# Top-two routing: one-hots laid out with the token tiles innermost, 16-bit operands, number tables repeated by GpSimd

## The chip, the cores and the metric

One core of one Trainium2 chip runs the whole program in one launch. The metric is the device time of one execution in microseconds, the median over the runs.

## The reference

The model is a chain of four gated attention layers, each followed by a gated feed-forward layer, over x of shape 2 x 1024 x 256. The change touches the last feed-forward layer, a mixture of 8 experts of which every token uses its best two:

```python
router_logits = x @ wg.T                       # 2048 tokens, 8 experts
probs = softmax(router_logits)
topk_w, topk_idx = top_k(probs, 2)
topk_w = topk_w / sum(topk_w)
expert_w = sum(one_hot(topk_idx, 8) * topk_w[..., None], axis=1)
h1 = einsum('th,eih->tei', x, w1)
h3 = einsum('th,eih->tei', x, w3)
y = einsum('tei,ehi->teh', silu(h1) * h3, w2)
out = einsum('te,teh->th', expert_w, y)        # then x = x + tanh(g_ffn[3]) * out
```

## The kernel before

All engines run hand-written programs that meet at semaphores; there is no planner. Each engine executes its list in the order written, and `then(...)` on VectorE marks an instruction whose result the next one waits for.

**The last attention.** `multihead` (called for layer 3, about 780 to 917 us in the profile) takes the 2048 tokens as NT = 16 tiles of P = 128 rows. An object `RouteAhead` rides along: it normalises finished rows, writes them to HBM as `xn_rows`, and computes the router's logits. At its start GpSimd clears a buffer (L696), computes the norm's powers (L373), and then writes small integer tables with `iota` (L1403 to L1407), a triangle (L1408) and zeros (L1410), in `gpsimd`. In `tables` VectorE turns the integer tables into 4-byte floats (L1418), while it works on attention tile 2. VectorE's instructions at L386 subtract and scale rows for the transposes at L475 on TensorE.

**The top-two stage.** `top2_ffn` runs when the logits are there. The two experts of each token split the work into 2 x 2048 assignments. These are sorted by expert into slots; 128 slots make one tile of work, and NTILE = 39 tiles always suffice, however the experts are chosen. For every assignment the kernel knows its slot number `slf`, split as tile `hi` (slot / 128) and lane `lo` (slot mod 128). One-hots turn the scatter into matrix products: `in_lane[p, n, t, :]` has a one at the lane of token (t, p) for its n-th expert, and `hot[p, n, t, :]` a one at its tile. VectorE makes `hot` (L2609, 2 x 16 x 39 = 1248 elements per partition), `in_tile` = `hot` times the token's number (L2612), and `in_lane` (L2616, four instructions of 8 tiles x 128 lanes = 1024 elements, each of which raises the semaphore `cells`). TensorE adds up the 32 products of `in_lane` (128 columns, the loaded operand) and `in_tile` (39 columns, the streamed one) in one PSUM tile (L2465); the sum holds at (lane, tile) the number of the token in that slot. For each product it waits for the `cells` of its group of eight.

```python
for n in range(TOP):
    for t in (0, 8):
        dve.tensor_tensor(in_lane[:, n, t:t + 8, :], lo[:, n, t:t + 8].unsqueeze(2).broadcast_to([P, 8, P]),
                          ahead.lane[:, :].unsqueeze(1).broadcast_to([P, 8, P]), ALU.is_equal).then_inc(cells, 1)
```

Behind `in_lane` VectorE computes which expert each tile belongs to (`cmp` L2619, `cnt` L2621, `te` L2622), and then `take` (L2625), the token numbers as indices. GpSimd waits for `take` and gathers the rows of a tile from HBM with indirect DMAs (L2424); `give` (L2638) are the indices by which results are added back to the output (L2444). Between the two VectorE splits the gate weights into three bf16 parts (L2629, L2631) and makes the first of three products `in_w` = `hot` times a part (L2634). The other two follow after the first two gathered tiles were copied (L2642).

**The tiles.** Each of the 39 tiles is transposed by TensorE (L2471), copied, multiplied with w1 and w3 of its expert (L2480, in 4-byte floats, eight records per tile), passed through silu on ScalarE (L2546), multiplied on VectorE (L2653), transposed again (L2488), multiplied with w2 (L2495), scaled by its weight and scattered. Tile 0 runs alone. Behind its products with w1 and w3 TensorE makes 32 products of `in_lane` and `in_w` (L2525, 3 x 39 = 117 columns), which bring the weights to the slots; VectorE reads them (L2680 to L2682). Then a loop runs over the rest, in pairs of tiles.

The printed functions are those that the diff touches.

Of the kernel before, what the change touches and what calls it, by code (L numbers as in the profile page):

```python
# [24 lines left out]
P = 128  # L25
# [1342 lines left out]
class RouteAhead(GateAhead):  # L1368
# [3 lines left out]
    def __init__(self, nc, ctx, K, tag, E, gw, gw_in, xn_dram, out_rows):  # L1372
        super().__init__(nc, ctx, K, tag, E, gw, gw_in, xn_dram)
        self.out_rows = out_rows
        self.n_out = 9 * 16
        self.NTILE = (2 * B * S + E * (P - 1)) // P
        NTILE = self.NTILE
        self.rev_i = sbuf(nc, ctx, tag + "rev_i", [P, E], I32)
        self.rev = sbuf(nc, ctx, tag + "rev", [P, E])
        self.jrow_i = sbuf(nc, ctx, tag + "jrow_i", [P, NTILE], I32)  # L1380
        self.jrow = sbuf(nc, ctx, tag + "jrow", [P, NTILE])
        self.lane_i = sbuf(nc, ctx, tag + "lane_i", [P, P], I32)
        self.lane = sbuf(nc, ctx, tag + "lane", [P, P])
        self.tok_i = sbuf(nc, ctx, tag + "tok_i", [P, NT], I32)
        self.tok = sbuf(nc, ctx, tag + "tok", [P, NT])
        self.dump_i = sbuf(nc, ctx, tag + "dump_i", [P, 1], I32)
        self.dump = sbuf(nc, ctx, tag + "dump", [P, 1])
        self.tri = sbuf(nc, ctx, tag + "tri", [P, P])
        self.trib = sbuf(nc, ctx, tag + "trib", [P, P], BF16)
        self.onesb = sbuf(nc, ctx, tag + "onesb", [P, P], BF16)  # L1390
        self.ev = sbuf(nc, ctx, tag + "ev", [P, 3, E + 1])
        self.table, self.table_f = semaphores(nc, ctx, tag, "table table_f")
# [9 lines left out]
    def gpsimd(self, pool):  # L1402
# [7 lines left out]
        pool.memset(self.ev[:, :, :], 0.0).then_inc(self.table, 1)  # L1410
        super().gpsimd(pool)

    def tables(self, dve):
        dve.wait_ge(self.table, 7)
        for f, i in ((self.rev, self.rev_i), (self.jrow, self.jrow_i), (self.tok, self.tok_i), (self.dump, self.dump_i),
                     (self.lane, self.lane_i), (self.trib, self.tri),
                     (self.onesb, self.K.ones)):
            dve.tensor_copy(f[:, :], i[:, :]).then_inc(self.table_f, 1)  # L1418
# [946 lines left out]
def top2_ffn(nc, ctx, K, tag, ahead, layer, w1, w3, w2, n_up, w2_loads):  # L2365
# [9 lines left out]
    with ExitStack() as r:  # L2375
# [11 lines left out]
        lo = sbuf(nc, r, tag + "lo", [P, TOP, NT])  # L2387
        gwt = sbuf(nc, r, tag + "gwt", [P, 3, TOP, NT])
        part = sbuf(nc, r, tag + "part", [P, 3, TOP, NT], BF16)
        in_lane = sbuf(nc, r, tag + "in_lane", [P, TOP, NT, P], F16)  # L2390
        in_tile = sbuf(nc, r, tag + "in_tile", [P, TOP, NT, NTILE], F16)
        hot = sbuf(nc, r, tag + "hot", [P, TOP, NT, NTILE], BF16)
        in_w = sbuf(nc, r, tag + "in_w", [P, TOP, NT, 3, NTILE], BF16)
# [19 lines left out]
        with nc.Block() as block:  # L2413
# [36 lines left out]
            def _(pe):  # L2450
# [11 lines left out]
                for n in range(TOP):  # L2462
                    for t in range(NT):
                        pe.wait_ge(cells, 2 * n + t // 8 + 1)
                        m = pe.matmul(ps[:, SLOT, 0:NTILE], in_lane[:, n, t, :], in_tile[:, n, t, :],  # L2465
                                      start=(n == 0 and t == 0), stop=(n == TOP - 1 and t == NT - 1))
# [56 lines left out]
                for n in range(TOP):  # L2523
                    for t in range(NT):
                        m = pe.matmul(ps[:, WEIGHT, 0:3 * NTILE], in_lane[:, n, t, :],  # L2525
                                      in_w[:, n, t, :, :].rearrange("p a j -> p (a j)"),
                                      start=(n == 0 and t == 0), stop=(n == TOP - 1 and t == NT - 1))
# [27 lines left out]
            def _(dve):  # L2555
# [12 lines left out]
                dve.wait_ge(ahead.table_f, 7)  # L2568
# [35 lines left out]
                then(dve.tensor_scalar(hi[:, :, :], hi[:, :, :], MAGIC, MAGIC, ALU.add, ALU.subtract))  # L2604
                then(dve.scalar_tensor_tensor(lo[:, :, :], hi[:, :, :], -float(P), slf[:, :, :], ALU.mult, ALU.add))
                def cells_of(v, n):
                    return v.unsqueeze(3).broadcast_to([P, TOP, NT, n])

                then(dve.tensor_tensor(hot[:, :, :, :], cells_of(hi[:, :, :], NTILE),  # L2609
                                       ahead.jrow[:, :].unsqueeze(1).unsqueeze(1).broadcast_to([P, TOP, NT, NTILE]),  # L2610
                                       ALU.is_equal))
                s.did(dve.tensor_tensor(in_tile[:, :, :, :], hot[:, :, :, :],  # L2612
                                        ahead.tok[:, :].unsqueeze(1).unsqueeze(3).broadcast_to([P, TOP, NT, NTILE]), ALU.mult))
                for n in range(TOP):
                    for t in (0, 8):
                        dve.tensor_tensor(in_lane[:, n, t:t + 8, :], lo[:, n, t:t + 8].unsqueeze(2).broadcast_to([P, 8, P]),  # L2616
                                          ahead.lane[:, :].unsqueeze(1).broadcast_to([P, 8, P]),
                                          ALU.is_equal).then_inc(cells, 1)
# [14 lines left out]
                def weigh(a):  # L2633
                    return dve.tensor_tensor(in_w[:, :, :, a, :], hot[:, :, :, :], cells_of(part[:, a, :, :], NTILE), ALU.mult)  # L2634
# [192 lines left out]
```

## Time and profile before

| what | value |
|---|---|
| median of 3 runs | 1189.49 us (1184.92 to 1190.48) |
| profiled execution | 1189.43 us |
| its span between first and last instruction | 1187.5 us |
| mean granted TensorE clock | 0.91 of full speed |
| busy: TensorE | 1010.1 us, 85% of the span |
| busy: VectorE | 643.1 us, 54% |
| busy: ScalarE | 401.1 us, 34% |
| busy: GpSimd | 255.4 us, 22% |

The profile is of one execution. PE is TensorE's matmuls, PEld its weight loads (they run beside the matmuls), DVE is VectorE, ACT ScalarE, POOL GpSimd, SP the engine that issues most DMAs. Times of rows are microseconds from the span's start.
### The profile page before, as it was taken

The page shows a single profiled execution, that of the slowest core. Times are in us where ns is not written, and L with a number is a line of the kernel's source. Part 1 is how long each engine was busy: PE and PEld are TensorE (multiplying, and loading weights), DVE is VectorE, ACT ScalarE, POOL GpSimd, SP SyncE. Part 2 cuts the span into 40 slices and gives each one's busy share as a digit, 9 for nine tenths or more (in the row PEclk, how much of TensorE's full clock was granted, in tenths as well). Part 3 has the DMA queues.
Part 4 walks back from the last instruction along what each step waited for, and adds up shares of the span by engine and source line. Part 5 has one row for each costly group of instructions (what it writes and reads, how often), then busy time and mean ns, then how long its engine had stood idle before and what let it go on. Part 6 is the DMA issues. An engine that isn't in the chain of part 4 may idle for free. (4 is left out here: it accounts for less than half of the span.)

```text
span 1187.5 us, 16543 instructions
## 1 busy us (share of the span) xinstructions
PE 1010.1 (85%) x5500; PEld 779.0 (66%) x5501; DVE 643.1 (54%) x1271; ACT 401.1 (34%) x638; POOL 255.4 (22%) x243
## 2 busy tenths in 40 slices
PE   5899999699999996776749549889998499999995
PEld 3678878578888873555637438758786266666663
DVE  5668769911232138777633478855686633333332
ACT  2544412111111127866520058535453021212220
POOL 3000001124544334300000000110000134444442
PEclk8999989889999999889975569997999599999998
DMA  4600131036766530000010200008112422222231
GB/s 130 195 1 19 37 108 36 27 120 167 200 195 169 148 89 0 1 1 1 1 37 1 71 0 1 2 4 290 37 37 84 148 40 44 44 44 44 44 45 22
DMA packets 67812, 79.63 MB, mean 67 GB/s; under 512 B 12656, under 2 KB 52171, under 8 KB 67755
## 3 DMA queue, kind: packets, MB, share of 16 engines
q1 hardware_dynamic: 54123, 60.27, 15.3%
q0 software_dynamic: 13632, 18.62, 9.3%
q8 instruction: 34, 0.56, 0.2%
q14 instruction: 23, 0.19, 0.1%
HBM read 60.73 MB, written 17.83 MB: 66 GB/s over the span
## 5 line engine op out<-in xcount | busy, mean ns | idle before, releaser
L2480 PE MATMUL ps<-w_L_ffn_w,f_xsT 128*128 x312 | 149.6, 603 | 0.6 <-DVE f_xsT L2642 0.6
L2276 DVE TENSOR_TENSOR f_h<-f_h,ps 128x1024 f32<-128x1024 f32 x24 | 29.3, 1220 | 111.4 <-PE ps L2072 58.1
L2444 POOL DMA_INDIRECT out_x<-f_yo,f_give x39 | 61.9, 1588 | 122.6 <-DVE f_yo L2659 119.7
L373 POOL TENSOR_TENSOR norm_vec<-norm_vec,npow 128x4 f32<-128x4 f32 (+2 forms) x25 | 25.3, 1013 | 282.2 <-DVE norm_vec L367 281.3
L2480 PEld LDWEIGHTS ps<-w_L_ffn_w,f_xsT 128*128 128x128 f32 x312 | 57.2, 194 | 42.6 <-issue 40.7
L2081 PE MATMUL ps<-b_room,f_h 128*128 128x256 f32 x384 | 85.0, 379 | 0.0
L2546 ACT ACTIVATE f_s<-ps 128x512 f32<-128x512 f32 x39 | 23.3, 597 | 182.0 <-PE ps L2480 182.0
L2081 PEld LDWEIGHTS ps<-b_room,f_h 128*128 128x128 f32 x384 | 72.9, 190 | 9.9
L534 PE MATMUL ps<-a_vblk,a_pT 128*128 128x51 f32 (+1 forms) x640 | 77.2, 277 | 0.0
L534 PEld LDWEIGHTS ps<-a_vblk,a_pT 128*128 128x128 f32 (+1 forms) x640 | 76.5, 197 | 0.3 <-issue 0.2
L2495 PE MATMUL ps<-w_L_ffn_w,f_hT 128*128 x312 | 73.9, 380 | 0.9 <-DVE f_hT L2647 0.9
L2048 POOL DMA_INDIRECT acc_rows<-f_eo,f_idx x32 | 52.4, 1637 | 100.9 <-DVE f_eo L2305 52.4
L2171 ACT ACTIVATE f_h<-ps 128x1024 f32<-128x1024 f32 x24 | 24.6, 1023 | 119.3 <-PE ps L2064 119.3
L717 DVE TENSOR_REDUCE a_mx<-ps 128x16 f32<-128x1232 f32 x32 | 46.0, 1438 | 34.5 <-PE ps L504 20.2
L2064 PE MATMUL ps<-f_xgT,b_room 128*128 128x256 f32 x256 | 60.1, 389 | 2.8 <-ACT f_xgT L2193 2.8
L2495 PEld LDWEIGHTS ps<-w_L_ffn_w,f_hT 128*128 128x128 f32 x312 | 56.4, 190 | 8.1 <-issue 2.0
L2647 DVE COPY f_hT<-ps 128x512 f32<-128x512 f32 x39 | 27.0, 692 | 61.5 <-PE ps L2488 61.5
L2072 PE MATMUL ps<-f_xgT,b_room 128*128 128x256 f32 x256 | 57.9, 379 | 0.0
L2064 PEld LDWEIGHTS ps<-f_xgT,b_room 128*128 128x128 f32 x256 | 49.1, 195 | 11.1 <-issue 4.5
L2072 PEld LDWEIGHTS ps<-f_xgT,b_room 128*128 128x128 f32 x256 | 48.6, 190 | 6.6
L523 PE MATMUL ps<-ident,a_pr 128*128 128x128 f32 x320 | 49.2, 287 | 4.1 <-ACT a_pT L681 0.8
L2653 DVE TENSOR_TENSOR f_hid<-f_s,ps 128x512 f32<-128x512 f32 x39 | 26.8, 688 | 42.6 <-PE ps L2480 38.6
(376 smaller groups left out, 2099.4 us busy)
## 6 DMA issues: line engine op xcount, KB each, us to landing
w_L_ffn_w<-in_L_ffn_w SPq DMA_DIRECT2D x24, 512.0 KB, 8.2
b_room<-in_L_ffn_Wg SPq DMA_DIRECT2D x16, 512.0 KB, 4.7
b_room<-in_L_ffn_Wu SPq DMA_DIRECT2D x16, 512.0 KB, 6.1
b_room<-in_L_ffn_Wd SPq DMA_DIRECT2D x16, 512.0 KB, 5.9
xn_rows<-xn_sb SPq DMA_DIRECT2D x8, 512.0 KB, 2.9
x_sb<-in_x SPq DMA_DIRECT2D x4, 512.0 KB, 7.0
xn_sb<-in_L_ffn_w SPq DMA_DIRECT2D x2, 1024.0 KB, 7.8
x_sb<-acc_rows SPq DMA_DIRECT2D x4, 512.0 KB, 5.5
```

Of the source, the lines that this page charges most:

```text
L523: m = pe.transpose(ps[0:w, 4 + r % 2, (part - lo) * P:(part - lo + 1) * P], pr[:, n % 2, part * P:part * P + w], K.ident[:, :])
L534: m = pe.matmul(ps[:, 6, h * HV:(h + 3) * HV], pT[0:w, n % 2, part, :], vblk[0:w, n // TB, part, :, :].rearrange("p j c -> p (j c)"), star ...
L717: dve.tensor_reduce(mxt, sc, AX.X, ALU.max).then_inc(sh_step, 1)
L2048: pool.indirect_dma_start(acc_dram[:, :], bass.IndirectOffsetOnAxis(ap=idx[:, n:n + 1], axis=0), eo[e % 2][:, b, :], None, compute_op=ALU. ...
L2064: m = pe.matmul(ps[:, f // 2, (f % 2) * W:(f % 2 + 1) * W], g[:, k, f * P:(f + 1) * P], rhs[k], start=(k == 0), stop=(k == KT - 1))
L2072: m = pe.matmul(ps[:, 2 + f // 2, (f % 2) * W:(f % 2 + 1) * W], u[:, k, f * P:(f + 1) * P], rhs[k], start=(k == 0), stop=(k == KT - 1))
L2081: m = pe.matmul(ps[:, 4 + p, j * D:(j + 1) * D], hT[p][:, f, j * P:(j + 1) * P], w[:, f, :], start=(f == 0), stop=(f == FT - 1))
L2276: dve.tensor_tensor(hT[p][:, :, :].rearrange("p a c -> p (a c)"), ge[p][:, :], ps[:, 2:4, :].rearrange("p a c -> p (a c)"), ALU.mult).then ...
L2444: pool.indirect_dma_start(out_rows[:, :], bass.IndirectOffsetOnAxis(ap=give[:, j:j + 1], axis=0), yo[j % 2][:, :], None, compute_op=ALU.ad ...
L2480: m = pe.matmul(ps[:, banks[p], :], xsT[p][:, i * P:(i + 1) * P], w[:, e, i, :], start=(i == 0), stop=(i == KT - 1))
L2495: m = pe.matmul(ps[:, Y_BANK, 0:D], hT[p][:, f * P:(f + 1) * P], w2[:, e, f, :], start=(f == 0), stop=(f == FT - 1))
L2647: dve.tensor_copy(hT[p][:, :], ps[:, HT[p], :]).then_inc(ht_sb, 1)
```

## The change

The one-hots change the order of their dimensions: the 16 token tiles become innermost in `in_lane`, `in_tile`, `hot` and `in_w`, where the lanes or the 39 tiles were innermost. `lo` and the rounded tile number (now `tile_of`) become f16, and the number tables that they are compared with, `lanes`, `tiles` and `toks`, are f16 as well, with `lanes` and `tiles` repeated 16 times so that no operand repeats an element innermost. GpSimd writes these tables with three copies behind its tables in the last attention, after a wait for its own seven instructions; VectorE makes two small casts fewer there (`tok` and `lane`). `in_lane` is written by two instructions of 2048 elements in place of four of 1024, and TensorE waits for `cells` by halves. TensorE's operands in L2465 and L2525 are slices of one token tile: their columns now lie 16 elements, 32 bytes, apart.

```diff
@@ -1380,16 +1380,17 @@
         self.jrow_i = sbuf(nc, ctx, tag + "jrow_i", [P, NTILE], I32)
         self.jrow = sbuf(nc, ctx, tag + "jrow", [P, NTILE])
         self.lane_i = sbuf(nc, ctx, tag + "lane_i", [P, P], I32)
-        self.lane = sbuf(nc, ctx, tag + "lane", [P, P])
         self.tok_i = sbuf(nc, ctx, tag + "tok_i", [P, NT], I32)
-        self.tok = sbuf(nc, ctx, tag + "tok", [P, NT])
         self.dump_i = sbuf(nc, ctx, tag + "dump_i", [P, 1], I32)
         self.dump = sbuf(nc, ctx, tag + "dump", [P, 1])
         self.tri = sbuf(nc, ctx, tag + "tri", [P, P])
         self.trib = sbuf(nc, ctx, tag + "trib", [P, P], BF16)
         self.onesb = sbuf(nc, ctx, tag + "onesb", [P, P], BF16)
         self.ev = sbuf(nc, ctx, tag + "ev", [P, 3, E + 1])
-        self.table, self.table_f = semaphores(nc, ctx, tag, "table table_f")
+        self.lanes = sbuf(nc, ctx, tag + "lanes", [P, P, NT], F16)
+        self.tiles = sbuf(nc, ctx, tag + "tiles", [P, NTILE, NT], F16)
+        self.toks = sbuf(nc, ctx, tag + "toks", [P, NT], F16)
+        self.table, self.table_f, self.wide_f = semaphores(nc, ctx, tag, "table table_f wide_f")
 
     def sync(self, sp, x_done):
         sp.dma_start(self.out_rows[B * S:B * S + P, :], self.K.zeros[:, :]).then_inc(self.rows_out, 16)
@@ -1408,12 +1409,16 @@
         pool.affine_select(out=self.tri[:, :], in_=self.K.ones[:, :], compare_op=ALU.is_ge, fill=0.0, base=-1,
                            pattern=[[1, P]], channel_multiplier=-1).then_inc(self.table, 1)
         pool.memset(self.ev[:, :, :], 0.0).then_inc(self.table, 1)
+        pool.wait_ge(self.table, 7)
+        pool.tensor_copy(self.lanes[:, :, :], self.lane_i[:, :].unsqueeze(2).broadcast_to([P, P, NT])).then_inc(self.wide_f, 1)
+        pool.tensor_copy(self.tiles[:, :, :],
+                         self.jrow_i[:, :].unsqueeze(2).broadcast_to([P, self.NTILE, NT])).then_inc(self.wide_f, 1)
+        pool.tensor_copy(self.toks[:, :], self.tok_i[:, :]).then_inc(self.wide_f, 1)
         super().gpsimd(pool)
 
     def tables(self, dve):
         dve.wait_ge(self.table, 7)
-        for f, i in ((self.rev, self.rev_i), (self.jrow, self.jrow_i), (self.tok, self.tok_i), (self.dump, self.dump_i),
-                     (self.lane, self.lane_i), (self.trib, self.tri),
+        for f, i in ((self.rev, self.rev_i), (self.jrow, self.jrow_i), (self.dump, self.dump_i), (self.trib, self.tri),
                      (self.onesb, self.K.ones)):
             dve.tensor_copy(f[:, :], i[:, :]).then_inc(self.table_f, 1)
 
@@ -2384,13 +2389,14 @@
         vec = sbuf(nc, r, tag + "vec", [P, 8, NT])
         slf = sbuf(nc, r, tag + "slf", [P, TOP, NT])
         hi = sbuf(nc, r, tag + "hi", [P, TOP, NT])
-        lo = sbuf(nc, r, tag + "lo", [P, TOP, NT])
+        lo = sbuf(nc, r, tag + "lo", [P, TOP, NT], F16)
+        tile_of = sbuf(nc, r, tag + "tile_of", [P, TOP, NT], F16)
         gwt = sbuf(nc, r, tag + "gwt", [P, 3, TOP, NT])
         part = sbuf(nc, r, tag + "part", [P, 3, TOP, NT], BF16)
-        in_lane = sbuf(nc, r, tag + "in_lane", [P, TOP, NT, P], F16)
-        in_tile = sbuf(nc, r, tag + "in_tile", [P, TOP, NT, NTILE], F16)
-        hot = sbuf(nc, r, tag + "hot", [P, TOP, NT, NTILE], BF16)
-        in_w = sbuf(nc, r, tag + "in_w", [P, TOP, NT, 3, NTILE], BF16)
+        in_lane = sbuf(nc, r, tag + "in_lane", [P, TOP, P, NT], F16)
+        in_tile = sbuf(nc, r, tag + "in_tile", [P, TOP, NTILE, NT], F16)
+        hot = sbuf(nc, r, tag + "hot", [P, TOP, NTILE, NT], BF16)
+        in_w = sbuf(nc, r, tag + "in_w", [P, TOP, 3, NTILE, NT], BF16)
         empty = sbuf(nc, r, tag + "empty", [P, NTILE])
         wsum = sbuf(nc, r, tag + "wsum", [P, NTILE])
         cmp = sbuf(nc, r, tag + "cmp", [1, NTILE, E])
@@ -2461,8 +2467,8 @@
                 m.then_inc(rank_ps, 1)
                 for n in range(TOP):
                     for t in range(NT):
-                        pe.wait_ge(cells, 2 * n + t // 8 + 1)
-                        m = pe.matmul(ps[:, SLOT, 0:NTILE], in_lane[:, n, t, :], in_tile[:, n, t, :],
+                        pe.wait_ge(cells, n + 1)
+                        m = pe.matmul(ps[:, SLOT, 0:NTILE], in_lane[:, n, :, t], in_tile[:, n, :, t],
                                       start=(n == 0 and t == 0), stop=(n == TOP - 1 and t == NT - 1))
                 m.then_inc(slot_ps, 1)
                 def turn(p, there):
@@ -2522,8 +2528,8 @@
                 pe.wait_ge(w_rdy, 1)
                 for n in range(TOP):
                     for t in range(NT):
-                        m = pe.matmul(ps[:, WEIGHT, 0:3 * NTILE], in_lane[:, n, t, :],
-                                      in_w[:, n, t, :, :].rearrange("p a j -> p (a j)"),
+                        m = pe.matmul(ps[:, WEIGHT, 0:3 * NTILE], in_lane[:, n, :, t],
+                                      in_w[:, n, :, :, t].rearrange("p a j -> p (a j)"),
                                       start=(n == 0 and t == 0), stop=(n == TOP - 1 and t == NT - 1))
                 m.then_inc(w_ps, 1)
                 pe.wait_ge(w2_in, 16 * len(w2_loads))
@@ -2565,7 +2571,7 @@
                 def per_expert(v):
                     return v.unsqueeze(1).broadcast_to([P, NT, E])
 
-                dve.wait_ge(ahead.table_f, 7)
+                dve.wait_ge(ahead.table_f, 5)
                 dve.wait_ge(ahead.l_ps, 1)
                 logits = ps[:, ahead.LOGITS, :].rearrange("p (i c e) -> p c i e", i=4, c=4)[:, :, :, 0:E]
                 split = tmp[:, 0, :, :].rearrange("p (c i) e -> p c i e", c=4)
@@ -2601,21 +2607,21 @@
                                        tmp[:, 0, :, :].unsqueeze(1).broadcast_to([P, TOP, NT, E]), ALU.mult))
                 then(dve.tensor_reduce(slf[:, :, :], at[:, :, :, :], AX.X, ALU.add))
                 then(dve.tensor_scalar(hi[:, :, :], slf[:, :, :], 1.0 / P, (P - 1.0) / (2 * P), ALU.mult, ALU.subtract))
-                then(dve.tensor_scalar(hi[:, :, :], hi[:, :, :], MAGIC, MAGIC, ALU.add, ALU.subtract))
-                then(dve.scalar_tensor_tensor(lo[:, :, :], hi[:, :, :], -float(P), slf[:, :, :], ALU.mult, ALU.add))
-                def cells_of(v, n):
-                    return v.unsqueeze(3).broadcast_to([P, TOP, NT, n])
-
-                then(dve.tensor_tensor(hot[:, :, :, :], cells_of(hi[:, :, :], NTILE),
-                                       ahead.jrow[:, :].unsqueeze(1).unsqueeze(1).broadcast_to([P, TOP, NT, NTILE]),
-                                       ALU.is_equal))
+                then(dve.tensor_scalar(tile_of[:, :, :], hi[:, :, :], MAGIC, MAGIC, ALU.add, ALU.subtract))
+                then(dve.scalar_tensor_tensor(lo[:, :, :], tile_of[:, :, :], -float(P), slf[:, :, :], ALU.mult, ALU.add))
+
+                def in_cells(v):
+
+                    return v.unsqueeze(2).broadcast_to([P, TOP, NTILE, NT])
+
+                dve.wait_ge(ahead.wide_f, 3)
+                then(dve.tensor_tensor(hot[:, :, :, :], in_cells(tile_of[:, :, :]),
+                                       ahead.tiles[:, :, :].unsqueeze(1).broadcast_to([P, TOP, NTILE, NT]), ALU.is_equal))
                 s.did(dve.tensor_tensor(in_tile[:, :, :, :], hot[:, :, :, :],
-                                        ahead.tok[:, :].unsqueeze(1).unsqueeze(3).broadcast_to([P, TOP, NT, NTILE]), ALU.mult))
+                                        in_cells(ahead.toks[:, :].unsqueeze(1).broadcast_to([P, TOP, NT])), ALU.mult))
                 for n in range(TOP):
-                    for t in (0, 8):
-                        dve.tensor_tensor(in_lane[:, n, t:t + 8, :], lo[:, n, t:t + 8].unsqueeze(2).broadcast_to([P, 8, P]),
-                                          ahead.lane[:, :].unsqueeze(1).broadcast_to([P, 8, P]),
-                                          ALU.is_equal).then_inc(cells, 1)
+                    dve.tensor_tensor(in_lane[:, n, :, :], lo[:, n, :].unsqueeze(1).broadcast_to([P, P, NT]),
+                                      ahead.lanes[:, :, :], ALU.is_equal).then_inc(cells, 1)
                 then(dve.tensor_tensor(cmp[:, :, :], ev[0:1, 2, 1:E + 1].unsqueeze(1).broadcast_to([1, NTILE, E]),
                                        ahead.jrow[0:1, :].unsqueeze(2).broadcast_to([1, NTILE, E]), ALU.is_le))
                 then(dve.tensor_reduce(cnt[:, :], cmp[:, :, :], AX.X, ALU.add))
@@ -2631,7 +2637,7 @@
                         then(dve.tensor_tensor(gwt[:, a + 1, :, :], gwt[:, a, :, :], part[:, a, :, :], ALU.subtract))
 
                 def weigh(a):
-                    return dve.tensor_tensor(in_w[:, :, :, a, :], hot[:, :, :, :], cells_of(part[:, a, :, :], NTILE), ALU.mult)
+                    return dve.tensor_tensor(in_w[:, :, a, :, :], hot[:, :, :, :], in_cells(part[:, a, :, :]), ALU.mult)
 
                 weigh(0)
                 then(dve.tensor_scalar(empty[:, :], of_slot, 0.0, ahead.dump[:, 0:1], ALU.is_equal, ALU.mult))
```

## Rows read from the trace of the kernel before

**Rows 1.** Windows: busy us per engine (x instructions), granted clock, DMA share, GB/s.

```profile
780.00:917.00 137.00, 125.69 (x975) 99.35 (x975) 88.03 (x183) 66.90 (x133) 9.40 (x15) 0.94 0.28 95
917.00:941.00 24.00, 5.14 (x71) 3.72 (x70) 18.57 (x47) 1.50 (x2) 3.31 (x3) 0.50 0.55 187
941.00:950.00 9.00, 8.52 (x42) 4.57 (x42) 4.10 (x6) 0.60 (x1) 1.88 (x2) 0.65 0.09 31
950.00:1170.00 220.00, 219.96 (x829) 135.89 (x830) 82.90 (x152) 45.78 (x56) 92.40 (x71) 1.00 0.28 43
```

**Rows 2.** Chain of waits, 917 to 956 us: start, us, what.

```profile
926.14 1.47 DVE f_hot L2609
...
927.63 1.46 DVE f_in_tile L2612
929.09 4.54 DVE f_in_lane L2616 x4
...
934.72 0.11 DVE f_take L2625
...
935.66 1.13 POOL f_xs L2424
...
937.10 2.98 DMA f_xs<-xn_rows,f_take
...
941.43 6.58 PE ps L2480 x8
...
948.23 1.73 PE ps L2525 x32
...
952.02 0.44 PE ps L2488 x4
952.46 1.72 PE ps L2480 x4
```

**Rows 3.** Groups by form, 905 to 956 us: line, shapes, count, busy us, mean ns.

```profile
L2616 DVE TENSOR_TENSOR f_in_lane<-f_lo,g_lane 128x1024 f16<-128x1024 f32 x4 | 4.6, 1218 | 0.0
L2634 DVE TENSOR_TENSOR f_in_w<-f_hot,f_part 128x1248 bf16<-128x1248 bf16 x3 | 4.3, 1454 | 0.0
...
L2465 PE MATMUL ps<-f_in_tile,f_in_lane 128*128 128x39 f16 x32 | 1.8, 203 | 8.8 <-DVE f_in_lane L2616 8.8
```

**Rows 4.** Timeline, 926 to 936 us, TensorE: start, us, instructions, [idle before <-releaser].

```profile
933.69 0.45 PE L2465 MATMUL ps<-f_in_tile,f_in_lane 128*128 128x39 f16 x8 [0.69 <-DVE f_in_lane L2616]
```

**Rows 5.** Groups by form, VectorE, whole span.

```profile
L1627 DVE TENSOR_SCALAR f_va<-xn_sb,f_wv 128x2048 f32<-128x2048 f32 x2 | 2.6, 1276 | 0.0
...
L1632 DVE SCALAR_TENSOR_TENSOR f_q<-xn_sb,f_wv,f_va 128x2048 fp32r<-128x2048 f32 x1 | 2.3, 2342 | 0.0
...
L2609 DVE TENSOR_TENSOR f_hot<-f_hi,g_jrow 128x1248 bf16<-128x1248 f32 x1 | 1.5, 1460 | 0.0
```

**Rows 6.** Timeline, 779 to 840 us: GpSimd, VectorE, TensorE; start, us, instructions.

```profile
779.84 0.90 POOL L696 MEMSET a_vblk<- 128x960 f32 x1 [9.16 <-POOLq L1006]
...
779.88 0.93 DVE L751 COPY a_vblk<-own 128x30 f32<-128x30 f32 x2 [0.31 <-PEq L1006]
...
785.75 1.73 DVE L386 TENSOR_SCALAR xn_sb<-x_sb,norm_vec  x4
785.76 0.12 POOL L1410 MEMSET g_ev<- 128x27 f32 x1
...
791.67 1.04 PE L475 MATMUL ps<-ident,xn_sb 128*128 128x128 f32 x8
...
839.39 1.01 POOL L373 TENSOR_TENSOR norm_vec<-norm_vec,npow 128x4 f32<-128x4 f32 x1 [53.51 <-DVE norm_vec L367]
```

**Rows 7.** Groups by form, GpSimd, whole span.

```profile
L1668 POOL TENSOR_SCALAR f_h<-f_h,f_vec 128x256 f32<-128x256 f32 x16 | 18.1, 1144 | 13.2 <-ACT f_h L1662 13.2
L2027 POOL TENSOR_TENSOR f_eo<-f_eo,x_sb 128x512 f32<-128x512 f32 x6 | 7.6, 1265 | 60.6 <-ACT f_eo L2185 60.6
```

## The prediction

> **What bounds the kernel now.** I began with the windows view, cut at the stages around the change [rows 1]. Three stretches matter. In the last attention (780 to 917 us) TensorE is busy 125.69 of 137 us. From 950 to 1170 us, the loop over the expert tiles, it is busy 219.96 of 220 us at a granted clock of 1.00: whatever makes the loop start earlier makes the kernel end earlier by as much, and whatever lengthens TensorE's work there lengthens the kernel. Between them, from 917 to 941 us, TensorE works 5.14 of 24 us and VectorE 18.57: here VectorE's chain is the bound, and it is the place of the change.
>
> The chain of waits then shows which instructions stand on it [rows 2]. The comparison for `hot` (1.47 us), the product `in_tile` (1.46) and the four comparisons for `in_lane` (4.54) follow each other on VectorE. Then come the tile numbers `te`, then `take` at 934.72, the first gathers on GpSimd, a landing, and TensorE at 941.43. Nothing in this chain runs beside something longer, so a microsecond taken from it before 934 us is a microsecond of the kernel. Further on, the 32 weight products of line 2525 stand on the chain with 1.73 us, between the first tile and the loop.
>
> **The change, part by part.**
>
> *VectorE's one-hots on the chain.* An instruction of 1024 elements takes 1218 ns and one of 1248 takes 1454 to 1460 [rows 3, 5]: about one element per step, also where all three operands are 16 bits wide, as in line 2634. That instruction repeats one number along its innermost dimension; after the change no operand does. Line 1627, with one source, takes 1276 ns for 2048 elements where a two-source instruction takes 2342 [rows 5], so the engine has a double pace, but no row shows it with two sources. The bounds are therefore no gain and half the steps. I take half, because the difference between line 2634 and the new form is exactly the repeated innermost element. Then `in_lane` needs two instructions of as many steps as two of the present four: 4.54 / 2 = 2.27 us saved. `hot` and `in_tile` each lose 624 steps; at (1460 - 1218) / 224 = 1.08 ns per step that is 0.67, and I write 0.65 each. On the chain: 2.27 + 0.65 + 0.65 = **-3.57 us**.
>
> The Trainium skill, "VectorE: DVE Perf Modes", section "The perf-mode tier table", gives 1224 ns for a bf16 `tensor_tensor` of 2048 elements, and asks for 16-bit operands with a step of one in the innermost dimension; the trace agrees in its negative half, line 2634, and shows no positive case. By that figure the two new `in_lane` instructions would take 2.4 us.
>
> *The other one-hots.* The three `in_w` products get shorter in the same way. The first lies between `take` and `give`, beside the gathers (1.13 us of issue, 2.98 to land); the other two lie beside the first tile's 6.58 us of TensorE work [rows 2]. They are worth nothing; even if the first tile ran in half its time, they would end before it.
>
> *The slot products, line 2465.* Eight pairs of load and matmul take 0.45 us, one alone 0.203 [rows 3, 4], so a pair costs (0.45 - 0.20) / 7 = 36 ns. TensorE now waits for a whole `in_lane` instruction: 16 pairs, not 8, stand behind the last one. They are hidden up to a point: `in_lane` ends at 929.09 + 4.54 = 933.63 and `take` starts at 934.72, 1.09 us later, because `te` comes first [rows 2]. Today's last pairs begin at 933.69 [rows 4]. Sixteen would end 0.06 + 0.20 + 15 x 0.036 = 0.80 us after `in_lane`: hidden.
>
> *Strided reads by TensorE.* Both operands of lines 2465 and 2525 now step by 16 elements, 32 bytes, from column to column. No row shows such a read. The low bound is no cost. For the high bound I take the 4-byte pairs of line 2480: four passes of 512 columns in 1.72 us [rows 2] are 0.84 ns per column, two passes per matmul 1.68, so 117 columns take 197 ns against 1.73 / 32 = 54 now, a factor of 3.6. The nearest row in size is line 2488: four 128-column 4-byte pairs in 0.44 us, 110 ns each, a factor of 2. I take 2, since a step that breaks the sharing of one fetch between neighbours resembles wider elements more than it resembles 512 columns. Line 2525 then costs 1.73 us more, all of it on the chain. Line 2465 at 72 ns a pair ends 0.06 + 0.20 + 15 x 0.072 = 1.34 us after `in_lane`; with 0.05 for the hand-over, `take` is 0.30 later. Together **+2.03 us**.
>
> The Trainium skill, "Advanced Engine Details and Errata", section "Memory Cachelines", says that SBUF is read in lines of 16 bytes and that a line must be hit at least twice in succession for full speed, which speaks against this change: with 32 bytes between columns every column is a line of its own. It gives no figure for TensorE, and no row here tests it; without its penalty the sum would be -3.57.
>
> *GpSimd's number tables.* Three copies, 2048 + 624 + 16 = 2688 elements, go behind the memset that ends at 785.88; GpSimd's next work is at 839.39 [rows 6]. At the memset's pace (0.90 / 960) they last 2.5 us; at that of line 2027 (1265 / 512) 6.6; at that of line 1668 (1144 / 256) 12.0 [rows 6, 7]. GpSimd has 53 us for it. But while the memset ran, a VectorE copy of 30 elements took 0.93 us and ended with it: the two engines can hold each other up. VectorE has 1.73 us of work at 785.75, which TensorE needs at 791.67. So (791.67 - 785.88 - 1.73) = 4.06 us are free; the copy is a one-source instruction, and I take 2.5: **0**. VectorE makes two small casts fewer in an attention that TensorE bounds: 0. No DMA, and nothing on SP's queue, changes.
>
> Sum: -3.57 + 2.03 = **-1.5 us** against the profiled execution, 1189.43 us (span 1187.5 and 1.9 around it), which stands at the median of the runs, 1189.49. That gives **1187.9 us**.
>
> **The rivals.**
>
> *A, the strided reads are free.* Against: 32 bytes between columns. For: nothing in the trace says they cost. Then -3.57, 1185.9 us.
>
> *B, the strided reads give back more than VectorE saves (slower).* With a pair's factor f, the weight products cost 1.73 (f - 1) and the slot products delay `take` by 0.54 f - 0.78; this passes 3.57 at f = 2.7, that is 144 ns for a pair of line 2525. At the high bound of 3.6 the costs are 4.5 + 1.2, the net is +2.1 and the time 1191.5; were it 6, beyond every row here, 8.65 + 2.46 - 3.57 = +7.5, 1197.
>
> *C, VectorE does not take the double pace.* Then the instructions keep their steps, the cost of 2.03 stays, and the time is 1191.5. For: no two-source row runs at it. Against: the engine has it, and the one obstacle visible is removed.
>
> *D, GpSimd's copies hold VectorE up in the attention.* From 1.51 ns per element on (4.06 / 2688) TensorE waits at 791.67; at 6.6 us for the copies it waits 2.5, at 12.0 us 7.9. Net +1.0 to +6.4: up to 1195.8.
>
> *E, TensorE's clock rises at another point.* The granted clock is 0.50 over 917 to 941 and 0.65 over 941 to 950 [rows 1]: the first tile's eight passes take 6.58 us where the loop needs 2 x 1.72 [rows 2]. An earlier start of that tile can meet the rise sooner (at best 3.1 us) or later (the weight products and the next pass, 1.73 + 1.98, half of it lost or 1.9). I take no change.
>
> **How the numbers follow.** Chances: my forecast 0.45, A 0.20, B 0.15, C 0.10, D 0.05, E 0.05. A difference of 0.5%, 5.9 us, is about what a measurement of this kernel can tell from none; the three runs shown are 5.6 us apart. Faster by more than that (under 1183.5) needs A together with an early clock or with the scatter of runs: 0.09. Slower by more (over 1195.4) needs the far end of B or D: 0.05. The rest, 0.86, is no difference to be measured. Range: A less 2 us of scatter, 1183.9, up to B's bound by rows with 0.9 us of scatter, 1192.5.
>
> **What would show it.** In the profile after: `in_lane` as two VectorE instructions of about 1.2 us, `hot`, `in_tile` and `in_w` near 0.8 us (1.45 would be C). The 32 weight products in about 3.5 us (1.7 would be A, over 4.6 B). `take` about 1.1 to 1.4 us after the last `in_lane`. The GpSimd copies in about 2.5 us at 786, and TensorE's transposes still at 791.7 (else D). The loop itself unchanged, 219.96 busy of 220. I am wrong if the stretch from 917 us to the loop's start is not shorter by 1 to 4 us, or if the time moves elsewhere.

## The result and the profile after

The changed kernel takes 1194.82 us (median of 5 runs, 1190.50 to 1195.52) against 1188.68 of the kernel before in the same measurement. The measured ratio is 1.0039, 95% interval 1.0021 to 1.0056; it is not the quotient of the two medians, which lie 6.1 us or 0.5% apart, and the same holds for the ratios below. The kernel is slower by about 0.4%, where 1.5 us less were forecast. The span of the profiled execution is 1192.8 us.

Lines of the changed kernel are shifted: 2471 is the slot products' 2465, 2486 the 2480, 2494 the 2488, 2531 the 2525 of before; in most experiments they stand 3 lines further on (2474, 2489, 2497, 2534), and with the tables alone at 2473, 2488, 2496 and 2533.

VectorE did what was forecast. The timeline of the router stage after (start, us, engine, line; idle time and its releaser in brackets), for rows 2 and 4:

```profile
929.19 0.81 DVE L2618 TENSOR_TENSOR f_hot<-f_tile_of,g_tiles 128x1248 bf16<-128x1248 f16 x1
930.03 0.81 DVE L2620 TENSOR_TENSOR f_in_tile<-f_hot,g_toks 128x1248 f16<-128x1248 bf16 x1
930.76 2.35 DVE L2623 TENSOR_TENSOR f_in_lane<-f_lo,g_lanes 128x2048 f16<-128x2048 f16 x2
...
932.03 2.73 PE L2471 MATMUL ps<-f_in_tile,f_in_lane 128*128 128x39 f16 x32 [5.47 <-DVE f_in_lane L2623]
...
934.80 0.20 DVE L2631 TENSOR_SCALAR f_take<-ps 128x39 uint32<-128x39 f32 x1 [0.60 <-PE ps L2471]
```

`hot` and `in_tile` take 0.81 us each, and the two `in_lane` instructions end at 930.76 + 2.35 = 933.11. From the start of `hot` that is 3.92 us; before it was 7.49 [rows 2]. The difference is 3.57 us, as forecast.

What was gained is lost behind it. `take` no longer waits for `te` but for the slot products: 32 of them in 2.73 us, and `take` 1.69 us after the last `in_lane` where it was 1.09. Then the chain of waits after, from GpSimd's first gather on:

```profile
935.83 1.14 POOL f_xs L2430
...
937.27 2.73 DMA f_xs<-xn_rows,f_take
...
941.37 6.10 PE ps L2486 x8
...
947.68 6.99 PE ps L2531 x32
954.67 2.68 PE ps L2486 x4
957.35 0.44 PE ps L2494 x4
957.79 1.72 PE ps L2486 x4
```

Ahead of the gather this view does not go on to `take`: it puts GpSimd's wait down to the sync engine and, behind it, to the loads of the experts' weights, which landed at 935.05. GpSimd's program waits there for the rows written to HBM in the last attention and for `take`, not for these weights, and from the end of `take` to the gather it is 0.83 us (935.00 to 935.83) as before (934.83 to 935.66). So I read the path through `take`, as in rows 2; that is an inference from the program and from this equal step.

The 32 weight products stand there with 6.99 us where they took 1.73 [rows 2], and the next pass of line 2486 with 2.68 where it took 1.98. That row of the chain of waits before:

```profile
950.04 1.98 PE ps L2480 x4
```

The groups by form show that it is not the work that grew, but the time of each record:

```profile
L2531 PE MATMUL ps<-f_in_w,f_in_lane 128*128 128x117 bf16 x32 | 7.2, 398 | 0.0
...
L2623 DVE TENSOR_TENSOR f_in_lane<-f_lo,g_lanes 128x2048 f16<-128x2048 f16 x2 | 2.4, 1218 | 0.0
L2640 DVE TENSOR_TENSOR f_in_w<-f_hot,f_part 128x1248 bf16<-128x1248 bf16 x3 | 2.3, 802 | 0.0
```

A pair of the weight products takes 6.99 / 32 = 218 ns, four times the 54 of before. And the clock: the windows view after (busy us of TensorE, its loads, VectorE, ScalarE, GpSimd; then the granted clock),

```profile
947.00:950.00 3.00, 3.00 (x16) 1.95 (x15) 1.02 (x2) 0.00 (x0) 0.94 (x1) 1.00 0.00 0
950.00:953.00 3.00, 3.00 (x16) 2.00 (x15) 0.00 (x0) 0.00 (x0) 0.00 (x0) 1.00 0.17 44
953.00:957.00 4.00, 4.00 (x12) 2.19 (x11) 0.59 (x3) 0.00 (x0) 0.00 (x0) 0.57 0.00 0
957.00:960.00 3.00, 3.00 (x14) 1.75 (x12) 1.15 (x2) 1.88 (x2) 0.00 (x0) 1.00 0.00 0
```

shows the products running at the full clock up to 953 us, with TensorE busy all the time, and then mostly the lower level, 0.57 on average from 953 to 957 us. In the kernel before, the clock stayed at 1.00 once it had risen there.

On the path, against rows 2: -3.57 (VectorE), +0.60 (`take`), +5.26 (weight products), +0.70 (the pass behind them at the lower clock) is +3.0 us. Up to the end of that pass the profiles differ by (957.35 - 929.19) - (952.02 - 926.14) = +2.28; the 0.7 between is the first tile, 6.10 us after and 6.58 before, and the gathers, 2.73 and 2.98 (the run with `in_w` back shows where their 0.25 comes from). The rest of the 5.3 us between the two spans lies ahead of the change, where `hot` starts 3.05 us later: 2.78 of it is there when the last attention starts (GpSimd's line 696 at 782.62, before at 779.84), 6 us before the first table copy. Over all the profiles this start scatters between 778.20 and 784.99. The loop is the same in both.

### The profile page after: what moved, and what is told of

It is laid out like the page before. It is cut to its first block and busy times, and to the rows that moved or that the text cites. A ratio compares the mean times of both kernels' runs of the same rounds, so it can differ in the third digit from the quotient of the medians.

```text
span 1192.8 us, 16543 instructions
## 1 busy us (share of the span) xinstructions
PE 1021.2 (86%) x5500; PEld 788.8 (66%) x5501; DVE 638.6 (54%) x1267; ACT 401.9 (34%) x638; POOL 258.1 (22%) x246
## 5 line engine op out<-in xcount | busy, mean ns | idle before, releaser
L2176 ACT ACTIVATE f_h<-ps 128x1024 f32<-128x1024 f32 x24 | 24.6, 1024 | 117.4 <-PE ps L2069 117.4
```

## The experiments

Theory 1: TensorE streams columns slowly when they lie far apart, and the clock falls behind that. The rivals: the loaded operand's step costs as well or alone; GpSimd's table copies lengthen the attention; the earlier stages grew for another reason.

**Only the streamed operands strided.** `in_lane` has its lanes innermost, as before the change:

```diff
+        self.GL, self.GT = 1, 16
...
-        in_lane = sbuf(nc, r, tag + "in_lane", [P, TOP, P, NT], F16)
-        in_tile = sbuf(nc, r, tag + "in_tile", [P, TOP, NTILE, NT], F16)
...
+        GL, GT = ahead.GL, ahead.GT
+        NL, NG = NT // GL, TOP * NT // GT
+        in_lane = sbuf(nc, r, tag + "in_lane", [P, TOP * NL, P, GL], F16)
+        in_tile = sbuf(nc, r, tag + "in_tile", [P, NG, NTILE, GT], F16)
...
```

GL and GT are the numbers of token tiles that stand innermost in the loaded operand (`in_lane`) and in the streamed ones (`in_tile`, `in_w`, and `hot` with them). The cut lines (`...`) bring `hot`, `in_w`, the number tables and TensorE's slices to the same form; the next experiments change these two numbers alone.

> Only the streamed operands (in_tile, in_w) keep the token tiles innermost, 32 bytes between columns; in_lane has its lanes innermost again. Theory 1 (the streamed operand's step is what costs): the 32 weight products take about 7 us as in the changed kernel (218 ns a pair), the slot products about 80 ns a pair. Theory 2 (the loaded operand's step costs as well, or alone): the weight products take well under 7 us, down to 1.7. On VectorE in_lane goes back to about 2.2 us per 2048 elements, hot, in_tile and in_w stay at 0.8.

1195.85 us in one run. The chain of waits of this kernel, and from its timeline the last 16 slot products:

```profile
947.35 6.81 PE ps L2534 x32
954.16 3.41 PE ps L2489 x4
957.57 0.85 PE ps L2497 x4
```

```profile
934.02 1.33 PE L2474 MATMUL ps<-f_in_tile,f_in_lane 128*128 128x39 f16 x16 [0.87 <-DVE f_in_lane L2625]
```

The whole loss is there: 213 ns a pair, and behind it the lower clock: 3.41 us for the pass that takes 1.72 in the loop, 0.85 for the transposes that take 0.44. The slot pairs take (1.33 - 0.25) / 15 = 72 ns (80 were expected) at the lower clock for 39 columns, the weight pairs, mostly at the full clock, 213 ns for 117: 1.8 ns per column both times, with half or full clock alike (in the windows view the granted clock is 0.50 from 931.5 to 936 us and 1.00 from 945.0 to 951.75).

**Only the loaded operand strided.** `in_lane` as changed; `hot`, `in_tile` and `in_w` with the 39 tiles innermost:

```diff
+        self.GL, self.GT = 16, 1
...
```

> Only the loaded operand (in_lane) keeps the token tiles innermost; in_tile, hot and in_w have the 39 tiles innermost again and their VectorE instructions take 1.45 us again. Theory 1: 54 ns a pair in the weight products (1.73 us), 36 ns in the slot products, so the stage ends about 2.3 us earlier than before. Theory 2: the weight products take clearly more than 1.73 us, with a pair at 100 ns or more.

1187.03 us in one run. The chain, and the slot products from the timeline:

```profile
945.65 2.03 PE ps L2534 x32
947.68 1.90 PE ps L2489 x4
```

```profile
930.78 2.32 PE L2474 MATMUL ps<-f_in_tile,f_in_lane 128*128 128x39 f16 x32 [6.76 <-DVE f_in_lane L2625]
```

The loaded operand's step is not free: 63 ns for a weight pair where it was 54, (2.32 - 0.23) / 31 = 67 for a slot pair where it was 36. On the weight products that is little. On the slot products it is 31 ns a pair, nearly as much as the 36 that the streamed operand's step costs there (72 for 36), so theory 1, which had 36 ns for them, did not hold for these. From `hot` to `take` it is 6.50 us, before 8.58: 2.1 us less, where 2.3 were expected. Theory 2's "100 ns or more" did not come. The clock does not fall behind the weight products.

**How far apart is too far.** The token tiles in groups of 8, 4 and 2 innermost, in both operands; here for 8, the other widths alike:

```diff
+        self.GL, self.GT = 8, 8
...
```

> As the changed kernel, but with only 8 token tiles innermost: 16 bytes between columns instead of 32. VectorE as in the changed kernel (808 ns for hot). If the cost is one of lines of 16 bytes that are hit once, it is all still there: about 7 us for the weight products. If it grows with the distance, about half of the 5.3 us of extra time goes.

1193.89 us in one run. Its chain:

```profile
946.99 6.82 PE ps L2534 x32
953.81 2.73 PE ps L2489 x4
```

Nothing is won: 16 bytes between columns cost as much as 32.

> Four token tiles innermost: 8 bytes between columns, two columns to 16 bytes. At 4 bytes the products were free, at 16 they cost all. Theory 1 (what matters is whether a 16-byte piece is hit more than once): the weight products take 1.8 us, ratio to before 0.996 as with two tiles. Rival (the cost grows with the distance between 4 and 16 bytes): they take 3 us or more.

1185.18 us against 1190.17, ratio 0.9946, interval 0.9924 to 0.9969. Its chain:

```profile
949.62 3.48 PE ps L2534 x32
953.11 1.72 PE ps L2489 x4
```

The rival held, theory 1 did not: 109 ns a pair, twice the price of adjacent columns and half of that at 16 bytes, though every 16-byte piece is hit twice. The price grows from 4 to 16 bytes and then stays. The clock stayed up behind it. The slot products, at the lower clock, hardly paid: its timeline has 16 of them in 0.82 us with 0.21 for one, 41 ns a pair for 36.

> As the changed kernel, but with two token tiles innermost: 4 bytes between columns. VectorE's double pace should hold (inner run of 2 elements, 808 ns for hot, 1.2 us per 2048 elements of in_lane). Theory 1 and 2 alike: a column shares its 16 bytes with three neighbours, so the weight products go back to 1.73 us, 54 ns a pair. Then the stretch from hot to the loop is 3.6 us shorter than before and the kernel about 3.5 us faster than before, ratio 0.997. If VectorE needs a longer inner run, hot takes 1.46 us and nothing is gained.

1184.06 us (four runs) against 1188.86, ratio 0.9958, interval 0.9942 to 0.9975: faster than before. Its chain:

```profile
929.14 0.82 DVE f_hot L2620
...
929.98 0.81 DVE f_in_tile L2622
930.78 2.27 DVE f_in_lane L2625 x2
...
934.14 0.11 DVE f_take L2635
...
940.63 5.70 PE ps L2489 x8
...
946.55 1.78 PE ps L2534 x32
...
948.40 1.98 PE ps L2489 x4
```

VectorE keeps its double pace with an inner run of only two elements, and the weight products cost 56 ns a pair. From the start of `hot` to the end of that pass it is 950.38 - 929.14 = 21.24 us, before 25.88; of the 4.64, 0.88 belong to the first tile (5.70 for 6.58), so 3.76 to the layout (0.25 of them to the gathers, 2.73 us for 2.98).

**The changed kernel again, and its parts alone.** Four kernels were timed beside each other on one chip.

> The changed kernel once more, for a sharper ratio on the chip of the next three. Theory 1 (the streamed operand's step, and the lower clock that TensorE falls to behind the slow products): on the path -3.6 us on VectorE, +0.6 at take, +5.3 for the weight products, +0.7 to 2 for the clock: 3 to 5 us slower than before, ratio 1.003 to 1.004. Rival (something in the earlier stages grows as well, which the first profile showed as 2.8 us ahead of the change): ratio 1.005 or more, with the last attention again starting near 782.6 and not spread over 779 to 785.

1192.39 us against 1188.62, ratio 1.0034, interval 1.0019 to 1.0049: the loss is confirmed, 2.3 to 5.8 us. The chain of this profile:

```profile
938.63 5.35 PE ps L2486 x8
...
944.20 6.99 PE ps L2531 x32
951.19 3.41 PE ps L2486 x4
954.60 0.85 PE ps L2494 x4
955.46 1.87 PE ps L2486 x4
```

The weight products are the same 6.99 us; the lower clock behind them costs more this time, 1.43 + 0.41 + 0.15 = 2.0 us. The first tile was shorter, 5.35. The rival does not hold, since the ratio stays under 1.005 and the start scatters: VectorE's first instruction of the router stage (it was at 917.86 us before and 920.92 after) is at 918.17 here, and over the profiles of this case it lies between 915.93 and 923.26, the first in the kernel with the tables alone, the last in the one with four tiles.

```diff
 # the kernel before, and in it:
+        pool.wait_ge(self.table, 7)
+        pool.tensor_copy(self.lanes[:, :, :], self.lane_i[:, :].unsqueeze(2).broadcast_to([P, P, NT])).then_inc(self.wide_f, 1)
...
```

> The kernel before with GpSimd's three copies of number tables alone, which nobody reads. Theory 1: the copies last 3 us beside the attention and hold VectorE's row shifts for 1.6 us, inside their slack; ratio 1.000, within 0.001. Rival (the copies cost part of the loss): ratio 1.002 or more, and the attention, from its first memset to the router's logits, longer by 2 us.

1188.46 us, ratio 0.9991, interval 0.9973 to 1.0010. The tables cost nothing that can be told. Its chain has the router stage as before:

```profile
924.20 1.47 DVE f_hot L2617
...
939.52 5.92 PE ps L2488 x8
...
945.67 1.72 PE ps L2533 x32
```

In the changed kernel the timeline of the attention shows why:

```profile
788.53 3.32 DVE L386 TENSOR_SCALAR xn_sb<-x_sb,norm_vec  x4
...
788.73 1.95 POOL L1413 CAST g_lanes<-g_lane_i 128x2048 f16<-128x2048 int32 x1
...
789.24 5.36 PE L484 MATMUL ps<-xnT_sb,w_L_xattn_w_q 128*128 128x512 f32 x8 [0.78 <-ACT xnT_sb L621]
...
794.44 1.04 PE L475 MATMUL ps<-ident,xn_sb 128*128 128x128 f32 x8
```

The copies take 1.95 us and less, and while they run VectorE's four row shifts last 3.32 us, not 1.73 [rows 6]. But TensorE asks for the rows only at 794.44, 5.20 us after its projection began, exactly as before (791.67 - 786.47, the second from the timeline before):

```profile
786.47 5.37 PE L484 MATMUL ps<-xnT_sb,w_L_xattn_w_q 128*128 128x512 f32 x8 [0.78 <-ACT xnT_sb L621]
```

The expectation named 2 us more for this stage as the rival. From GpSimd's line 696 to VectorE's first instruction of the router stage it is 132.7 us with the tables alone, 138.0 before and 138.3 after: the stage did not grow. The slack can be smaller than it looks here: with the tables alone TensorE came to the rows 3.51 us after the start of its projection, at 793.35, and the row shifts had ended at 792.45.

```diff
-        in_w = sbuf(nc, r, tag + "in_w", [P, TOP, 3, NTILE, NT], BF16)
+        in_w = sbuf(nc, r, tag + "in_w", [P, TOP, NT, 3, NTILE], BF16)
...
-                                      in_w[:, n, :, :, t].rearrange("p a j -> p (a j)"),
+                                      in_w[:, n, t, :, :].rearrange("p a j -> p (a j)"),
...
```

> As the changed kernel, but in_w has the 39 tiles innermost again, so that only the loaded operand of the 32 weight products keeps its step (VectorE's three in_w instructions take 1.45 us or more, beside the gathers). Theory 1: the weight products take about 2.0 us, the clock stays up behind them, take stays about 0.6 late; in all 2.5 us faster than before, ratio 0.998. Rival (the loss comes from elsewhere): still slower than before.

1187.56 us against 1188.62, ratio 0.9980, interval 0.9963 to 0.9996: this one part undone turns the loss into a small gain. VectorE's `in_w` from the groups by form, and the weight products from the chain:

```profile
L2640 DVE TENSOR_TENSOR f_in_w<-f_hot,f_part 128x1248 bf16<-128x1248 bf16 x3 | 7.1, 2393 | 0.0
```

```profile
948.69 1.99 PE ps L2531 x32
```

The products take 1.99 us. `in_w` now reads `hot` with 32 bytes between elements and takes 2393 ns where it took 1454 [rows 3]. That is not beside the chain altogether. The landing of the second gather on the chain here, and the issue of the second gather from the timelines, here and in the changed kernel:

```profile
937.79 3.86 DMA f_xs<-xn_rows,f_take
```

```profile
937.79 2.11 POOL L2430 DMA_INDIRECT f_xs<-xn_rows,f_take  x1 [0.30 <-issue]
...
937.27 0.96 POOL L2430 DMA_INDIRECT f_xs<-xn_rows,f_take  x1 [0.30 <-issue]
```

The first `in_w` product runs from 936.73 to 939.11 us, and the gather's issue, 2.11 us in place of 0.96, ends behind it. Over the ten profiles whose chain goes through this gather the piece takes 2.69 to 2.75 us where `in_w` takes 0.80, 2.98 to 3.02 where it takes 1.45, and 3.86 here. So the shorter `in_w` of the change is worth 0.25 us on the path, and this layout costs 1.1 us there. The only edit of this run is `in_w`, so the longer piece comes from it; that VectorE holds GpSimd's issue up is the likeliest mechanism, and it was not tested apart.

**Two token tiles, and `take` ahead of `te`.** The version with two token tiles innermost, with one more edit:

```diff
+                dve.wait_ge(slot_ps, 1)
+                of_slot = ps[:, SLOT, 0:NTILE]
+                dve.tensor_scalar(take[:, :], of_slot, -1.0, 0.0, ALU.add, ALU.max).then_inc(take_rdy, 1)
                 then(dve.tensor_tensor(cmp[:, :, :], ev[0:1, 2, 1:E + 1].unsqueeze(1).broadcast_to([1, NTILE, E]),
...
-                dve.wait_ge(slot_ps, 1)
-                of_slot = ps[:, SLOT, 0:NTILE]
-                dve.tensor_scalar(take[:, :], of_slot, -1.0, 0.0, ALU.add, ALU.max).then_inc(take_rdy, 1)
```

> Two token tiles innermost, as in the run that was faster than before, and take moved ahead of the three instructions for te, which only TensorE's first tile needs 6 us later. The slot products end about 0.85 us after the last in_lane, so take starts near 0.9 instead of 1.09 us after it: 0.2 us more than with te first. Ratio to before 0.996; against the version with te first not to be told apart by time, only by the rows.

1183.69 us against 1188.62, ratio 0.9954, interval 0.9936 to 0.9972. VectorE's timeline:

```profile
926.45 2.35 DVE L2625 TENSOR_TENSOR f_in_lane<-f_lo,g_lanes 128x2048 f16<-128x2048 f16 x2
929.61 0.20 DVE L2631 TENSOR_SCALAR f_take<-ps 128x39 uint32<-128x39 f32 x1 [0.81 <-PE ps L2474]
```

`take` starts 929.61 - 928.80 = 0.81 us after the last `in_lane`, near the expected 0.9 and 0.28 sooner than with `te` first. In time this kernel, the one with two tiles and the one with four can't be told apart; their intervals overlap, and each was timed against the kernel before on another chip.

One measure over all profiles takes the scatter ahead of the change out: from the start of `hot` to the end of the span. The first tile's eight passes, which begin at the lower clock, stand beside it.

| kernel | `hot` at | span | from `hot` to the end | first tile |
|---|---|---|---|---|
| before | 926.14 | 1187.5 | 261.4 | 6.58 |
| tables alone | 924.20 | 1185.1 | 260.9 | 5.92 |
| changed | 929.19 | 1192.8 | 263.6 | 6.10 |
| changed again | 926.45 | 1190.7 | 264.3 | 5.35 |
| streamed operands alone | 927.91 | 1193.8 | 265.9 | 5.17 |
| 8 tiles innermost | 928.65 | 1192.2 | 263.6 | 6.03 |
| loaded operand alone | 926.64 | 1185.1 | 258.5 | 5.48 |
| `in_w` back | 929.71 | 1188.3 | 258.6 | 5.47 |
| 4 tiles | 931.54 | 1190.1 | 258.6 | 6.48 |
| 2 tiles | 929.14 | 1185.9 | 256.8 | 5.70 |
| 2 tiles, `take` first | 924.88 | 1182.2 | 257.3 | 6.51 |

Without the first tile, which scatters, the third column less the fourth is 254.8 us before, 257.5 and 258.9 in the two profiles of the changed kernel, 251.1 with two tiles and 250.8 with `take` first. The losses of 2.7 and 4.1 us agree with the path: +3.0 and, with the longer stay at the lower clock in the second profile, +4.3, each less the 0.25 of the gathers.

## Why the prediction was wrong

The forecast was 1187.9 us, 1.5 less than before; the kernel became slower and came out at 1194.82, 2.3 us above the range. The step that failed is "Strided reads by TensorE", with its "I take 2". The factor for the weight products was 4.0 (218 ns for 54), above even the bound of 3.6 that I had taken from the 4-byte pairs. The reasoning behind the 2 was a likeness, that a step which breaks the sharing of a fetch resembles wider elements, and the row it leaned on, the 128-column pairs of line 2488, is of 4-byte numbers side by side: a strided 16-bit column costs 1.8 ns, more than the 1.68 of a 4-byte one. So the weight products cost +5.26 where the sum had +1.73.

Rival B named the right mechanism, and its own formula at f = 4.0 gives 3 x 1.73 + (0.54 x 4.0 - 0.78) - 3.57 = +3.0 us, 1192.4; I gave it 0.15 and let the range end at the bound. That this equals the +3.0 of the first profile is luck: the formula has 1.38 us for `take`, where 0.60 were measured, and nothing for the clock, which took 0.70.

Four smaller terms. `take` was 0.60 later where I had 0.30: a slot pair takes (2.73 - 0.26) / 31 = 80 ns, a factor of 2.2. It is less than four because these products run at the lower clock [rows 1], where a dense column costs 36 / 39 = 0.92 ns and not the 0.46 of the weight products at the full one, while a strided column costs 1.8 at both; one factor for both lines was wrong. The clock, rival E, moved in a way that I had not listed: not the point of its rise but a fall behind the slow products, 0.7 and 2.0 us in the two profiles of the changed kernel. The `in_w` products, put at nothing, brought 0.25 us on the path, through the gather beside the first of them. And that the loaded and the streamed operand would pay alike was silently assumed; in a weight pair the loaded one pays 9 ns and the streamed one 159, in a slot pair 31 and 36.

Right were: that VectorE takes the double pace once no operand repeats its innermost element (-3.57 us to the hundredth), that GpSimd's copies are hidden (2.5 us forecast, 1.95 + 0.75 + 0.26 measured), though they did hold VectorE's row shifts, 3.32 us for 1.73, and that the loop does not change. The row with which the prediction argued for such a hold (0.93 us beside the memset) is of two copies, not one. The two casts fewer were not tested apart. The Trainium skill's rule on lines of 16 bytes ("Advanced Engine Details and Errata", "Memory Cachelines") spoke against the change and was right in direction. It asks for at least two hits on a line; that two are enough is not borne out by the run with 8 bytes between columns: two columns to a line still took 109 ns a pair for 54 to 56, and the measurement decides.

The ratios, 1.0034 and 1.0039, are 4.0 to 4.6 us of 1188.6. The profiles give +2.7 and, with the longer stay at the lower clock (2.0 in place of 0.70), +4.0, inside both intervals.

## What to carry to other kernels

A layout that doubles VectorE's pace must be priced at the reader's end too: here 3.6 us on VectorE cost 5.9 on TensorE, most of it because its streamed operand came apart, and the clock took 0.7 to 2.0 more. In this kernel the double pace needed an innermost run of two 16-bit elements, no more; with two rows interleaved, not sixteen, TensorE paid next to nothing (56 ns a pair for 54). Where many columns stream past a loaded operand, the side that streams is the one to keep dense: in the 117-column pairs at the full clock its step cost 159 ns and the loaded one's 9. In the 39-column pairs at the lower clock the two cost about the same, 36 and 31. And price such a read at the clock that its stage has: the dense column costs twice as much at the lower one, the one with 32 bytes to its neighbour does not.

## What the runs showed of the hardware that I had not expected

- A streamed 16-bit column costs 0.46 ns (54 / 117) with neighbours adjacent, 0.48 at 4 bytes between columns (1.78 us for 32 x 117), 0.93 at 8 bytes, 1.82 at 16 and 1.82 to 1.87 at 32, all of them mostly or wholly at the full clock. From 4 to 16 bytes, and for the 1.87, the loaded operand was strided alike; the 1.82 at 32 bytes is the streamed one alone. At 32 bytes this is the same at either level of the clock: 72 ns for 39 columns at the lower, 213 for 117 mostly at the full.
- A pair whose loaded operand alone has 32 bytes between columns takes 63 ns with 117 streamed columns at the full clock and 67 with 39 at the lower, where the dense pairs take 54 and 36. That the load, not the stream, is then the longer part would fit both; it was not tested.
- TensorE's clock fell to its lower level in all four profiles in which the weight products took about 7 us, and each time 1.5 to 2.3 us before these products ended, though the records show the engine busy throughout; in the seven in which they took 3.5 us or less it did not. That the slow streaming is what lowers it is the likeliest reading; it was not tested apart.
- The first tile's eight passes took between 5.17 and 6.58 us in kernels where nothing in them differs, with the granted clock rising at another point of them. That and the 7.3 us of scatter ahead of the stage (915.93 to 923.26) are larger than most of what this change is about.
- VectorE, too, pays for a source with 32 bytes between 16-bit elements: 2393 ns for 1248 elements, 1454 without.
